# Moving the step projections of layer 0 from states 2 and 5 to states 5 and 8 of a pass, and the x and gate projections one place on

## The chip, the cores and the metric

The kernel runs on one core of a Trainium2 chip. The metric is the device time of one execution in microseconds, as the median of several runs. The engines are PE (TensorE, matmul), DVE (VectorE), ACT (ScalarE), POOL (GpSimd) and SP (SyncE, which here only issues DMAs). Each engine works through its own instruction list in the order written in the program, and waits on semaphores that other engines or DMAs raise.

## The reference, cut to what matters

The input is x of 8 images, 32 by 32 pixels, 192 channels. Two layers follow one another, each with a residual. The change touches layer 0 alone:

```
xz = groupnorm(x) @ W_in.T;  xc, z = split(xz)        # 384 channels each
xc = silu(depthwise_conv3x3(xc) + conv_b)
for each of 8 scan orders k (rows, columns, mirrored, reversed):
    x_dbl  = xs[k] @ x_proj_weight[k].T               # 12 step values, 16 B, 16 C per pixel
    delta  = softplus(dts @ dt_projs_weight[k].T + bias)   # 12 -> 384 channels
    h[t]   = exp(delta[t]*A) * h[t-1] + delta[t]*u[t]*B[t] # 16 states n, 1024 steps t
    y     += sum over n of h[t,n]*C[t,n]  + D*u
y = layernorm(y) * silu(z);  out = y @ W_out.T
```

The product dts @ dt_projs_weight is called step projection below, xs @ x_proj_weight the x projection, and the z half of the input projection the gate projection. Layer 1 is a scan of another form with four directions and isn't changed.

## The kernel before, in words

The images follow one another. Channels lie on the 128 partitions in J = 3 tiles, the 1024 pixels along the free axis, all in 32-bit floats. For layer 0 an image has 8 scans (i) of 3 tiles (j) of 16 states (n): 384 units, `UNITS`, numbered g. The 16 units of one (i, j) are a pass; an image has 24.

For each unit: SP fetches the row of B, broadcast to 128 partitions, into one of four buffers (`spread_row`, L312). POOL multiplies it with delta*u (`source`, L1043) into one of five buffers. ACT makes the decay exp(delta*A) in PSUM (`decay`, L825). DVE scans (`scan`, L1212). Then the state is multiplied by C: in 12 of 16 states by DVE (`weigh`, L1220), for which PE first spreads the row of C over the partitions in the two PSUM banks `WORK` (`spread_c`, L526); in states 2, 5, 8 and 11 (`by_pool`) by POOL (L1052), with a row of C that SP fetches. PE adds the product to the pass's sum by a matmul with the identity (`sum_states`, L556), and after a pass ACT copies the sum to y (`collect`, L831); at state 1 of the next pass PE reads y back into the sum (`begin_sums`, L544). In scan 0, DVE does that copy (L1225).

DVE's order is scan(g), then weigh(g-1) where that is DVE's. POOL's is source(g), then its weigh(g-3) where that is POOL's, and after source(6) of each pass `du` (L1033), two products that make delta*u of the next pass. POOL's source(g) waits for scan(g-5), whose buffer it takes, and for the row of B.

`WORK` is free in the four states whose C product is POOL's, since PE spreads no row for them. There PE does the projections, in pieces that `piece(g)` names. It is read by PE (`scans0` of the tensor block) at unit g, and by ACT at unit g+2, after decay(g+2), for the copy out of PSUM:

- ("dt", i, j): the step projection of the pass two on (`dt_proj`, L498; two matmuls of 12 rows and 512 columns, four in the trace), copied by `take_dt` (L802). Its softplus is at state 14.
- ("xd", i+1, q): a quarter of the next scan's x projection (`x_proj`), copied by `take_xd` (L777), after the fourth one `first_part`. The table `QUARTERS` has their places.
- ("rest", i+1, h): `remainders`, at states 8 and 11 of tile 2.
- ("z", j, h): the gate projection, in scan 7 alone. The table `GATES` has its places.

PE does a piece at unit g after it has waited for weigh(g-1), and before the sum of the state g-1 and the spread of g+1.

SP's list (`rows0`) goes by units too. At unit g it waits for source(g-4) to end and fetches B of g, and C of g if that is POOL's. At (0, 8) of scans 0 to 5, that is tile 0, state 8, after the rows of state 8, it waits for the step projection ("dt", i, 2) and then issues `load_wx(i + 2)`: two DMAs (L302, L303) which overwrite the weights that this projection was the last to read. At (2, 2) it stores the rows of the next scan's B and C to memory (`store_bc`).

Of the kernel before, what the change touches and what calls it, by code (L numbers as in the profile page):

```python
# [26 lines left out]
PASSES = K * J  # L27
# [25 lines left out]

QUARTERS = [(0, 5), (0, 8), (0, 11), (1, 2)]
GATES = {(0, 5): (0, 0), (0, 8): (0, 1), (0, 11): (1, 0), (1, 2): (1, 1), (1, 5): (2, 0), (1, 8): (2, 1)}


def last_xd(l, i):  # L60
# [4 lines left out]
def piece(g):  # L65

    if not 0 <= g < len(UNITS):
        return None
    i, j, n = UNITS[g]
    ahead = i * J + j + 2  # L70
    if n == (5 if j == 1 else 2) and ahead < PASSES:
        return "dt", ahead // J, ahead % J
    if i < K - 1 and (j, n) in QUARTERS:
        return "xd", i + 1, QUARTERS.index((j, n))
    if i < K - 1 and j == 2 and n in (8, 11):
        return "rest", i + 1, int(n == 11)
    if i == K - 1 and (j, n) in GATES:
        return "z", *GATES[j, n]
    return None
# [63 lines left out]
def program(nc, counts, images, x, out, w_in, conv_w, conv_b, w_x0, w_dt0, dt_b0, a_log0, d0,  # L143
# [3 lines left out]
    with ctx:  # L147
# [244 lines left out]
        def _(pe):  # L392
# [167 lines left out]
            def put_off(g):  # L560
                p = piece(g)
                return p is not None and p[0] == "rest"

            def scans0(b):
                for g in range(len(UNITS) + 1):
                    last = g - 1
                    if 0 <= last < len(UNITS) and not by_pool(*UNITS[last]):
                        pe.wait_ge(S["weigh"], at("weigh", UNITS[last], b))
                    p = piece(g)
                    if p:  # L570
                        if p[0] == "xd":
                            x_proj(b, p[1], p[2])
                        elif p[0] == "dt":
                            dt_proj(b, 0, p[1], p[2])
                        elif p[0] == "rest":
                            remainders(b, p[1], p[2])
                        else:
                            gate_projection(b, 0, p[1], p[2])
                    if g < len(UNITS) and not by_pool(*UNITS[g]):
                        spread_c(b, *UNITS[g])  # L580
                    if g >= SUM_LAG and by_pool(*UNITS[g - SUM_LAG]):
                        sum_states(b, g - SUM_LAG)

                    n = UNITS[g][2] if g < len(UNITS) else N
                    if n == 1:
                        begin_sums(b, last)
                    if n in (2, 3) or g >= 2 and put_off(g - 1):
                        sum_states(b, g - 2)
                    if 0 <= last and n not in (1, 2) and not put_off(g) and not by_pool(*UNITS[last]):
                        sum_states(b, last)  # L590
# [120 lines left out]
        def _(act):  # L711
# [121 lines left out]
            def scans0(b):  # L833
                for g in range(len(UNITS) + 2):
# [10 lines left out]
                    if g in (1, 2) and b > 0:  # L845
                        take_out1(b - 1, g - 1)
                    p = piece(g - 2)
                    if p and p[0] == "xd":
                        take_xd(b, 0, p[1], p[2])
# [627 lines left out]
```

## Time and profile before

| | us |
|---|---|
| median of 3 runs | 15642.82 |
| lowest and highest | 15638.57, 15650.55 |
| profiled execution: span from first to last instruction | 15638.3 |
| DVE busy | 14604.3 (93%) |
| POOL busy | 13820.4 (88%) |
| PE busy | 12948.2 (83%) |
| ACT busy | 8897.0 (57%) |
| DMA, share of 16 engines | 45.9% |
| mean granted TensorE clock | 0.946 |

The profile page gives no time for the profiled execution but its span; it lies within the three runs. Busy time is what an engine spends in instructions of its own. An image takes an eighth of the span; image 3 begins its layer 0 at 5912.1 and has 1222 us of it.

### The profile page before, as it was taken

Reading aid. Unit: us, or ns where it says so; the run is one execution under the profiler, and the core shown is the slowest. Engines: PE = TensorE matmul, PEld = TensorE weight load, DVE = VectorE, ACT = ScalarE, POOL = GpSimd, SP = SyncE. Lnnn points to the kernel's source line nnn. Section 1 sums busy time; section 2 is a strip of 40 time slices with the busy share of each in tenths; the row PEclk is TensorE's granted clock in tenths of the full one; section 3 lists DMA queues with packets and bytes.
Section 4 is the critical chain, followed back from the end, with each engine's and each line's share of the span. In section 5 each row is a group of like instructions: output and inputs, shape, how many; then the busy total and the mean of one; then the engine's idle time right before and its main releaser. Section 6 shows DMA issues by size and latency. Waiting matters only on the chain.

```text
span 15638.3 us, 128313 instructions
## 1 busy us (share of the span) xinstructions
PE 12948.2 (83%) x42560; PEld 7615.4 (49%) x42560; DVE 14604.3 (93%) x8593; ACT 8897.0 (57%) x8571; POOL 13820.4 (88%) x5892
## 2 busy tenths in 40 slices
PE   7887888878888788887888878888788887888878
PEld 4553355533555335553355533555335553355533
DVE  8998989989899899998999989999899998999988
ACT  4455745457454674556744567445674456744567
POOL 7997979979799798997989978899788997889978
PEclk8999999999999999999999999999999999999999
DMA  5662256622566225662256622566225662256622
GB/s 180 211 214 104 86 180 213 211 101 86 185 212 211 100 84 187 214 210 98 82 193 212 210 95 81 193 213 213 93 78 199 213 211 92 76 200 213 211 87 77
DMA packets 696921, 2473.06 MB, mean 158 GB/s; under 512 B 79292, under 2 KB 101064, under 8 KB 696264
## 3 DMA queue, kind: packets, MB, share of 16 engines
q1 hardware_dynamic: 696264, 2464.85, 45.9%
q8 instruction: 345, 5.65, 0.2%
q14 instruction: 312, 2.56, 0.1%
HBM read 2448.81 MB, written 15.73 MB: 158 GB/s over the span
## 4 chain that ended last, share of the span: by engine, by line
POOL 47%; issue 18%; DVE 13%; PE 11%; DMA 7%; ACT 3%; DVEq 0%; POOLq 0%; SPq 0%; ACTq 0%
POOL room L1043 24%; POOL room L1086 7%; DMA room<-bc_rows 7%; POOL room L1052 5%; POOL room L1078 4%; POOL room L1089 4%; DVE room L1279 4%; DVE room L1212 3%; PE bank L621 3%; POOL room L1033 3%; DVE room L1220 3%; PE bank L556 2%; PE bank L407 2%; DVE u L1169 1%; DVE room L1299 1%
## 5 line engine op out<-in xcount | busy, mean ns | idle before, releaser
L1043 POOL TENSOR_TENSOR room<-room 128x1024 f32<-128x1024 f32 x3072 | 7161.8, 2369 | 0.6
L1212 DVE TENSOR_TENSOR_SCAN room<-bank,room 128x1024 f32<-128x1024 f32 x3072 | 6936.5, 2278 | 75.7 <-POOL room L1043 71.7
L556 PE MATMUL bank<-room,identity 128*128 128x256 f32 x24576 | 5985.2, 389 | 188.5 <-DVE room L1220 188.5
L556 PEld LDWEIGHTS bank<-room,identity 128*128 128x128 f32 x24576 | 4758.9, 195 | 1333.5 <-DVE room L1220 269.6
L825 ACT ACTIVATE bank<-room,a 128x1024 f32<-128x1024 f32 x3072 | 3411.3, 1115 | 3273.9 <-DVE room L1212 3258.4
L621 PE MATMUL bank<-room,identity 128*128 128x512 f32 x6144 | 3011.5, 641 | 860.8 <-DVE room L1299 728.4
L1279 DVE TENSOR_TENSOR_SCAN room<-bank,room 128x1024 f32<-128x1024 f32 x1536 | 3431.5, 2274 | 54.1 <-POOL room L1086 33.6
L1220 DVE TENSOR_TENSOR room<-room,bank 128x1024 f32<-128x1024 f32 x2304 | 2764.1, 1200 | 387.3 <-PE bank L526 374.1
L621 PEld LDWEIGHTS bank<-room,identity 128*128 128x128 f32 x6144 | 1204.8, 204 | 2667.3 <-issue 1257.2
L1086 POOL TENSOR_TENSOR room<-room 128x1024 f32<-128x1024 f32 x768 | 2224.3, 2919 | 56.2 <-ACT room L908 26.7
L1052 POOL TENSOR_TENSOR room<-room 128x1024 f32<-128x1024 f32 x768 | 1817.1, 2366 | 344.1 <-DVE room L1212 343.0
L526 PE MATMUL bank<-parts,pick_row 96*128 96x512 bf16 x4608 | 1391.8, 383 | 806.7 <-DVE room L1220 702.4
L908 ACT ACTIVATE room<-room,a 128x1024 f32<-128x1024 f32 x1248 | 1365.9, 1138 | 4.5
L1089 POOL TENSOR_TENSOR room<-room 128x1024 f32<-128x1024 f32 x480 | 1160.5, 2428 | 0.0
L526 PEld LDWEIGHTS bank<-parts,pick_row 96*128 96x128 bf16 x4608 | 384.5, 99 | 1409.8 <-DVE room L1220 1079.0
L1033 POOL TENSOR_TENSOR room<-room,u 128x512 f32<-128x512 f32 x384 | 544.4, 1443 | 577.3 <-ACT room L808 577.3
L1078 POOL TENSOR_TENSOR room<-u,room 128x1024 f32<-128x1024 f32 x384 | 970.9, 2528 | 8.0 <-DMA room<-bc_rows 8.0
L600 PE MATMUL bank<-room,identity 128*128 128x512 f32 x1536 | 721.8, 592 | 0.0
L897 ACT ACTIVATE bank<-room,a 128x1024 f32<-128x1024 f32 x384 | 429.0, 1117 | 452.6 <-DVE room L1279 451.1
L498 PE MATMUL bank<-xdbl,wdt 12*128 12x512 f32 x864 | 488.1, 694 | 192.2 <-DVE room L1220 173.9
L1028 POOL TENSOR_TENSOR u<-room,u 128x1024 f32<-128x1024 f32 x24 | 56.6, 2356 | 651.3 <-ACT room L813 651.3
L918 ACT ACTIVATE bank<-room,a 128x1024 f32<-128x1024 f32 x288 | 320.6, 1113 | 383.6 <-DVE room L1279 383.6
(115 smaller groups left out, 8767.1 us busy)
## 6 DMA issues: line engine op xcount, KB each, us to landing
room<-bc_rows SPq DMA_DIRECT2D x4608, 512.0 KB, 4.4
wx<-in_w_x SPq DMA_DIRECT2D x65, 162.0 KB
bc_rows<-xdbl SPq DMA_DIRECT2D x72, 128.0 KB, 5.3
pictures<-in_x SPq DMA_DIRECT2D x8, 768.0 KB, 10.9
out_x<-pictures SPq DMA_DIRECT2D x8, 768.0 KB, 7.2
win<-in_w_in SPq DMA_DIRECT2D x16, 288.0 KB, 6.1
room<-in_w_in SPq DMA_DIRECT2D x16, 288.0 KB, 5.0
room<-in_w_out SPq DMA_DIRECT2D x16, 288.0 KB, 5.6
```

The lines of the kernel that those rows point to most:

```text
L526: ins = nc.tensor.matmul(bank[:, WORK[h], :], pick_row[:, N + n:N + n + 1].broadcast_to([XR, P]), parts[:, i % 2, halves(h)], start=True, ...
L556: ins = nc.tensor.matmul(dst[line][part], identity[:, :], src[line][part], start=(i == 0 and n == 0 and line == 0), stop=(n == N - 1 and l ...
L621: ins = nc.tensor.matmul(dst, identity[:, :], rhs, start=(q == 0), stop=(q == Q - 1))
L825: nc.scalar.activation(whole(DECAY0[g % 2]), delta0[:, j, :], ACT.Exp, scale=a0[:, col:col + 1]).then_inc(S["decay"], note("decay", (i, j, ...
L1043: nc.gpsimd.tensor_tensor(source0[:, g % SOURCES, :], du0[:, j, :], b_ring0[:, g % BROWS, :], ALU.mult).then_inc(S["source"], note("source ...
L1052: nc.gpsimd.tensor_tensor(state, state, c_ring0[:, c, :], ALU.mult).then_inc(S["weigh_pool"], note("weigh_pool", (i, j, n)))
L1078: nc.gpsimd.tensor_tensor(src, u[:, j, :], b_ring1[:, m % BROWS1, :], ALU.mult).then_inc(S["source1"], note("source1", (j, n)))
L1086: nc.gpsimd.tensor_tensor(state, state, src.rearrange("p (r c) -> p c r", r=SIDE), ALU.mult).then_inc(S["gated"], note("gated", (j, n, q)))
L1089: nc.gpsimd.tensor_tensor(state, state, src, ALU.mult).then_inc(S["gated"], note("gated", (j, n, q)))
L1212: nc.vector.tensor_tensor_scan(run(state0[:, g % STATES, :]), run(whole(DECAY0[g % 2])), run(source0[:, g % SOURCES, :]), 0.0, ALU.mult, A ...
L1220: nc.vector.tensor_tensor(state, state, whole(WORK[0]), ALU.mult).then_inc(S["weigh"], note("weigh", UNITS[g]))
L1279: nc.vector.tensor_tensor_scan(state, dec, state, 0.0, ALU.mult, ALU.add).then_inc(S["scan1"], note("scan1", (j, n, q)))
```

## The change

The step projections of tiles 0 and 2 go from state 2 to 5, that of tile 1 from 5 to 8. The quarters of the x projection and the six gate projections each go to the next place of the list. No computation is added or removed.

```diff
-QUARTERS = [(0, 5), (0, 8), (0, 11), (1, 2)]
-GATES = {(0, 5): (0, 0), (0, 8): (0, 1), (0, 11): (1, 0), (1, 2): (1, 1), (1, 5): (2, 0), (1, 8): (2, 1)}
+QUARTERS = [(0, 8), (0, 11), (1, 2), (1, 5)]
+GATES = {(0, 8): (0, 0), (0, 11): (0, 1), (1, 2): (1, 0), (1, 5): (1, 1), (1, 8): (2, 0), (1, 11): (2, 1)}
...
     ahead = i * J + j + 2
-    if n == (5 if j == 1 else 2) and ahead < PASSES:
+    if n == (8 if j == 1 else 5) and ahead < PASSES:
         return "dt", ahead // J, ahead % J
```

Places taken, by state, before and after:

| tile | before | after |
|---|---|---|
| 0 | 2 dt, 5 8 11 xd | 5 dt, 8 11 xd |
| 1 | 2 xd, 5 dt | 2 5 xd, 8 dt |
| 2 | 2 dt, 8 11 rest | 5 dt, 8 11 rest |

## Rows read from the trace of the kernel before

**Rows 1.** The page: busy engines, and one group of instructions with its idle time.

```profile
PE 12948.2 (83%) x42560; PEld 7615.4 (49%) x42560; DVE 14604.3 (93%) x8593; ACT 8897.0 (57%) x8571; POOL 13820.4 (88%) x5892
...
L1220 DVE TENSOR_TENSOR room<-room,bank 128x1024 f32<-128x1024 f32 x2304 | 2764.1, 1200 | 387.3 <-PE bank L526 374.1
```

**Rows 2.** Windows: stretch, its length, busy us of PE, PEld, DVE, ACT, POOL; clock; DMA.

```profile
6090.60:6839.10 748.50, 639.12 (x2580) 444.84 (x2580) 731.49 (x423) 373.57 (x380) 733.14 (x330) 0.98 0.62 212
...
6839.10:6989.30 150.20, 128.46 (x516) 89.46 (x516) 146.05 (x86) 77.11 (x79) 147.94 (x67) 0.98 0.61 211
...
8033.30:8788.10 754.80, 646.01 (x2580) 448.42 (x2580) 731.44 (x422) 373.44 (x380) 733.89 (x330) 0.97 0.61 210
...
6739.20:6787.90 48.70, 39.92 (x166) 28.24 (x166) 48.56 (x29) 24.72 (x25) 47.69 (x22) 1.00 0.61 211
```

**Rows 3.** Timeline of DVE, image 3, scan 5, tile 0: start, length, line, count.

```profile
6688.86 2.28 DVE L1212 TENSOR_TENSOR_SCAN room<-bank,room 128x1024 f32<-128x1024 f32 x1
...
6705.04 1.22 DVE L1220 TENSOR_TENSOR room<-room,bank 128x1024 f32<-128x1024 f32 x1 [1.78 <-PE bank L526]
...
6708.38 1.20 DVE L1220 TENSOR_TENSOR room<-room,bank 128x1024 f32<-128x1024 f32 x1
...
6735.91 2.28 DVE L1212 TENSOR_TENSOR_SCAN room<-bank,room 128x1024 f32<-128x1024 f32 x1
...
6739.22 2.28 DVE L1212 TENSOR_TENSOR_SCAN room<-bank,room 128x1024 f32<-128x1024 f32 x1
```

**Rows 4.** Timeline of POOL: the same pass, last row from scan 3.

```profile
6680.29 16.27 POOL L1043 TENSOR_TENSOR room<-room 128x1024 f32<-128x1024 f32 x7
6697.92 2.36 POOL L1052 TENSOR_TENSOR room<-room 128x1024 f32<-128x1024 f32 x1 [1.36 <-DVE room L1212]
...
6702.54 3.03 POOL L1033 TENSOR_TENSOR room<-room,u 128x512 f32<-128x512 f32 x2
...
6712.44 7.04 POOL L1043 TENSOR_TENSOR room<-room 128x1024 f32<-128x1024 f32 x3
...
6730.95 4.76 POOL L1043 TENSOR_TENSOR room<-room 128x1024 f32<-128x1024 f32 x2
...
6400.95 2.48 POOL L1033 TENSOR_TENSOR room<-room,u 128x512 f32<-128x512 f32 x2
```

**Rows 5.** Timelines of PE and SP, same pass, at state 2; then one window.

```profile
6698.99 1.97 PE L498 MATMUL bank<-xdbl,wdt 12*128 12x512 f32 x4 [0.59 <-DVE room L1220]
...
6700.99 0.33 SPq L302 DMA_DIRECT2D wx<-in_w_x  x1
...
6701.81 0.34 SPq L312 DMA_DIRECT2D room<-bc_rows  x1
...
6701.50:6704.50 3.00, 3.00 (x9) 2.25 (x8) 1.77 (x1) 2.65 (x3) 3.00 (x3) 0.55 0.73 145
```

**Rows 6.** State 5 of tile 1: timelines of DVE, PE (scan 5), then DVE elsewhere.

```profile
6756.85 1.20 DVE L1220 TENSOR_TENSOR room<-room,bank 128x1024 f32<-128x1024 f32 x1
...
6758.15 1.95 PE L498 MATMUL bank<-xdbl,wdt 12*128 12x512 f32 x4 [0.95 <-DVE room L1220]
...
318.57 1.22 DVE L1220 TENSOR_TENSOR room<-room,bank 128x1024 f32<-128x1024 f32 x1 [1.82 <-PE bank L526]
...
14251.38 1.22 DVE L1220 TENSOR_TENSOR room<-room,bank 128x1024 f32<-128x1024 f32 x1 [1.82 <-PE bank L526]
```

**Rows 7.** DMA view at the first row behind the weights: size, us to landing.

```profile
room<-bc_rows SPq DMA_DIRECT2D x1, 512.0 KB, 4.1
...
room<-bc_rows SPq DMA_DIRECT2D x1, 512.0 KB, 4.7
...
room<-bc_rows SPq DMA_DIRECT2D x1, 512.0 KB, 5.4
```

**Rows 8.** Timeline of DVE, image 3, scan 0, state 3 of tiles 1 and 2.

```profile
5998.55 1.22 DVE L1220 TENSOR_TENSOR room<-room,bank 128x1024 f32<-128x1024 f32 x1 [2.35 <-PE bank L526]
...
6055.61 1.22 DVE L1220 TENSOR_TENSOR room<-room,bank 128x1024 f32<-128x1024 f32 x1 [4.30 <-PE bank L526]
```

## The prediction

> **What bounds the kernel now.** I read the page first, then windows over whole scans, then the timelines of DVE, POOL, PE and SP side by side in one pass.
>
> The page shows DVE at 93% and POOL at 88% of the span, and one idle time of DVE that belongs to layer 0: 374.1 us in which the C product (L1220) waits for the spread row of C (L526) [rows 1]. The windows show how close the two engines are. Scan 6 of image 3 takes 150.20 us; DVE is busy for 146.05 of it and POOL for 147.94 [rows 2]. So layer 0 is bound by DVE plus 4.15 us of stalls for three passes, and POOL, which has only 2.26 us to spare, stands close behind. Whatever DVE gains beyond that, POOL takes back; and whatever delays POOL by more than its lead comes out at DVE.
>
> The timeline of one pass, scan 5, tile 0, shows the stall. The pass takes 6739.22 - 6688.86 = 50.36 us, with 1.78 in front of the product of state 3, so DVE's own pass is 48.58 [rows 3]. PE did the step projection from 6698.99 to 6700.96, and in the 3 us after 6701.50 its granted clock averaged 0.55, nearly all at the lower level, 1.2 GHz, after 0.59 us of idling and four matmuls of 12 rows [rows 5]. The sum of state 0 and the spread of state 3 come behind it on PE, at half speed. The pass with its step projection at state 5 took 48.70, with DVE busy 48.56: a stall of 0.14, its clock at 1.00 [rows 2]. So such a piece costs 0.14 at full clock and about 1.8 at half.
>
> POOL's own pass: source(15) of the pass before starts at 6680.29, so source(0) at 6682.60; source(15) starts at 6730.95, the next source(0) at 6733.26. Less 1.36 of waiting for scan(2), that is 49.3 us. `du` has 3.03 of it here and 2.48 in scans of rows and mirrored rows, where the pass is 48.8 [rows 4].
>
> **What the change removes.** The step projections at state 2 of tiles 0 and 2 go. In scans 3 to 6 nearly every one cost 1.78. With nothing at state 2, the spread of state 3 waits for the sum of state 0 alone, for which DVE leaves two scans' time: no stall. Tile 0 then goes to 48.6 for DVE before anything is added.
>
> **What it adds at states 5 and 8.** The same piece, of the same length, in front of the same sum and spread. The one before at state 5 of tile 1 is the nearest row: either 0.14, or 1.82 as in [rows 6]; of the 48 in scans 1 to 6 of eight images 15 had 1.82 (first and last shown). The bounds are none and all of them. I take 15 of 48, a share of 0.31, for every moved one, since it is the same place. DVE's passes:
> - tile 1: 48.58 + 0.14 = 48.7, below POOL's 48.8 or 49.3; or 48.58 + 1.82 = 50.4. Mean 0.69 x 48.8 + 0.31 x 50.4 = 49.3 in the first scans, and 49.6 with 49.3 for POOL in the later ones.
> - tile 2: scan 6 has 4.15 of stalls, of which 1.78 + 0.14 + 1.78 are step projections; 0.45 is left for the remainders. So 146.05 - 2 x 48.58 + 0.45 + 0.14 = 49.5, or 51.2; mean 50.0. Before it was 51.1 where halved.
>
> **What it adds on SP's queue.** This is the part that the diff doesn't show. At (0, 8) SP waits for the step projection of tile 2 before it issues the two weight loads, and all later rows of B and C queue behind that wait. Now PE ends it at 6700.96, SP issues the loads at 6700.99 and the row of state 9 at 6701.81 [rows 5], and source(9) starts at 6712.44 [rows 4]: hidden. Moved to state 5, the projection starts after weigh(4). Call the end of weigh(4) T. At state 5 of tile 1 the weigh ended at 6758.05 and the projection at 6760.10, so T + 2.05 [rows 6]. Then 0.03 to SP, 0.82 for two issues, and the landing of a row behind the weights: 4.7, the middle of the 55 rows of that kind, bounds 4.1 and 5.4 (shown are these three) [rows 7]. With 0.05 to wake, POOL can start source(9) at T + 7.65. Today it starts at 6712.44 - 6709.58 = T + 2.86 [rows 3, 4]; with T earlier by the 1.78 removed it would be about T + 4.6. So POOL loses 3 us here, more than its lead.
>
> From source(9) to source(15) are 18.51 us; scan(15) starts 2.41 later (2.36 for the source and 0.05), and the next scan(0) another 3.31 [rows 3, 4]. So the pass ends at T + 31.9, with T at 20.72 - 1.78 = 18.94 after scan(0): 50.8 us, where it now is 50.36 with a stall and 48.7 without. A halved clock at state 6 is hidden in it: scan(9) must wait to T + 10.1 anyway. The rows of states 10, 11 and 12 queue up too, but 213 GB/s at a share of 0.61 [rows 2] makes 1.5 us a row at full rate, faster than a source of 2.31.
>
> The Trainium skill ("DMA: Bandwidth & Descriptors", "Anatomy of one DMA") says that DMA engines don't wait on semaphores, the issuing sequencer does so before dispatch. The trace agrees: the row left SP only behind the loads.
>
> The same section puts a DMA at 2.0 us plus its bytes at 436 GB/s, fitted on the POOL-issued path; for 692 KB that is an estimate of 3.6 us rather than the 4.7 measured, and the sum below would be lower by 1.1 x 48 = 53 us, 15578. I go by the rows.
>
> **What else moves, at no cost.** The quarters of x at states 2 and 5 of tile 1: the pass that had a quarter at 2 and a step projection at 5 idled 0.14 in all, so a quarter costs nothing. ACT (57% busy) copies the step projection at state 7 or 10, before its softplus at 14, and no longer next to the copy of y at state 3. `store_bc` at (2, 2) waits for the last quarter, now at state 5 of tile 1, some 40 us ahead of use. If the ACT copy were late, it would show as a longer stall at the next product, at most one copy of 1.1 us.
>
> **The sum, for an image.** Scans 1 to 5 now: 748.50 in image 3 and 754.80 in image 4, mean 751.65 [rows 2]. After: scans 2 and 3, 50.8 + 49.3 + 50.0 = 150.1 each; scans 4 and 5, 50.8 + 49.6 + 50.0 = 150.4 each; scan 1 has DVE's last copy of y (731.49 - 5 x 146.05 = 1.2) more, 151.3. Together 752.3: +0.6. Scan 6 loads no weights: 49.6 + 49.6 + 50.0 = 149.2 for 150.2: -1.0. Scan 7, tile 0 alone: -0.8. Scan 0, tile 0: 31.9 from T for DVE's own 29.6, +2.3; tile 2: the stall of 4.30 [rows 8] goes, I put 0.3 in its place and 1.4 at state 5, where scan 0 halves more often, -2.6; tile 1 keeps its 2.35, for the quarter at state 2 stays. Sum 0.6 - 1.0 - 0.8 + 2.3 - 2.6 = -1.5, times 8 = -12 us. On the span of 15638.3 that is 15626; the median stands 4.5 above the span: 15631. The gain of about 3.4 us a scan from state 2 goes back to the new places of the stall and to SP's wait.
>
> **The rivals.**
> A. POOL's lead covers SP's wait, or the row comes much sooner. For: today's wait, equally long for the row, costs nothing. Against: T + 7.65 against T + 4.6. Then tile 0 would take 49.3 or 49.6 as tile 1 does: 1.5 less in scans 1 to 3, 1.2 in 4 and 5, 2.1 in 0; 9.0 an image, 72 us: 15559.
> B. The clock halves behind every moved projection, as it did in nearly all at state 2 of scans 3 to 6. Place: the products of state 9 in tile 1 and state 6 in tile 2. Price: tile 1 +1.1 or +0.8, tile 2 +1.1; in scans 1 to 5 4.8 + 5.7, in 6 and 7 3.5, so 14 an image, 112 us: 15743, slower. It decides from a share of about 0.57 on, where the time passes 15674. For: PE is emptier before state 5 than when a quarter stood at 2. Against: 33 of 48 at state 5.
> C. It halves behind none of them: tile 1 -0.5 or -0.3, tile 2 -0.5, in all 6.2 an image, 50 us: 15581.
> D. The row lands at 5.4: +0.7 x 48 = 34 us, 15665; at 4.1 29 us less.
>
> **How the numbers follow.** Forecast 0.47, A 0.12, B 0.18, C 0.18, D 0.05. What a measurement here can tell is 0.2%, 31 us. Faster (below 15612): A, C and 0.05 of the forecast's spread, 0.35. Slower (above 15674): B, 0.04 of the spread and most of D, 0.25. Same: 0.40. The forecast's own range, shares from 0.1 to 0.5 and landings of 4.4 to 5.0: 15595 to 15665. To leave out no more than 2 in 10 it goes down to 15562, just above A, and up to 15710, within B.
>
> **What would show it.** No stall in front of the product of state 3 in scans 2 to 6; stalls of 0.14 or 1.8 at state 6 of tile 2 and 9 of tile 1; in tile 0 of scans 0 to 5 POOL idle in front of source(9) until a row lands, 7.6 after weigh(4), and DVE then idle in front of scans 9 to 15 behind L1043, which it hardly is now. SP's weights 2.1 after weigh(4). Passes of 50.8, 49 and 50. It is wrong if POOL isn't idle there (A), or if PE's clock is low behind most of the moved pieces (B) or none (C).

## The result, and the profile after

The changed kernel is slower: 15706.36 us (median of 4 runs, 15697.92 to 15717.71) against 15645.6 for the kernel before (4 runs). The ratio is 1.0041, with a 95% interval of 1.0027 to 1.0054: 61 us lost where I forecast 12 gained. The time lies inside my range, but the likeliest case, no measurable change, did not happen. The profiled execution took 15714.33 us, 1.8 more than its span.

The page of the changed kernel, its span and four groups of instructions (busy us, mean ns, idle us and what ended most of it). The line of the engines and the one of L1220 answer to [rows 1]. Behind them stand three lines of the kernel before that [rows 1] doesn't show.

```profile
span 15712.5 us, 128298 instructions
...
PE 12977.8 (83%) x42560; PEld 7639.7 (49%) x42560; DVE 14626.1 (93%) x8593; ACT 8895.7 (57%) x8571; POOL 13818.4 (88%) x5892
...
L1043 POOL TENSOR_TENSOR room<-room 128x1024 f32<-128x1024 f32 x3072 | 7155.4, 2363 | 188.5 <-DMA room<-bc_rows 155.6
L1212 DVE TENSOR_TENSOR_SCAN room<-bank,room 128x1024 f32<-128x1024 f32 x3072 | 6940.8, 2277 | 138.1 <-POOL room L1043 72.8
...
L1220 DVE TENSOR_TENSOR room<-room,bank 128x1024 f32<-128x1024 f32 x2304 | 2759.0, 1197 | 379.9 <-PE bank L526 366.7
...
L1052 POOL TENSOR_TENSOR room<-room 128x1024 f32<-128x1024 f32 x768 | 1814.5, 2363 | 234.1 <-DVE room L1212 232.5
```
```profile
L1043 POOL TENSOR_TENSOR room<-room 128x1024 f32<-128x1024 f32 x3072 | 7161.8, 2369 | 0.6
L1212 DVE TENSOR_TENSOR_SCAN room<-bank,room 128x1024 f32<-128x1024 f32 x3072 | 6936.5, 2278 | 75.7 <-POOL room L1043 71.7
...
L1052 POOL TENSOR_TENSOR room<-room 128x1024 f32<-128x1024 f32 x768 | 1817.1, 2366 | 344.1 <-DVE room L1212 343.0
```

Two things are seen at once. POOL's sources, which had waited 0.6 us in all, now wait 188.5, and 155.6 of it is put down to a row that a DMA brings. POOL gets 110 of this back at its own C products (L1052), where it now waits 234.1 in place of 344.1: a part of the new wait only takes the place of an old one. At DVE the idle time before the scans (L1212) grew from 75.7 to 138.1. POOL is named for only 72.8 of it, for 71.7 before; of the added 62 us 40.1 stand as "issue" and 18.9 behind ACT's decay (L825), below as waits with us in total, times and longest. The 1.05 in front of scan(9) in the timeline further down is such an "issue": source(9) had ended just before, so the name is a weak guide there.

```profile
DVE room L1212 <- issue: 40.1, 70, 2.1
DVE room L1212 <- ACT bank L825: 18.9, 54, 1.0
```

And the wait of DVE for the spread row, 374.1 us before, is 366.7: the stall that the change was to shorten is still there, only in other places. Nearly the same amount of it, plus a new wait, is most of the result.

Windows of the changed kernel: scans 1 to 5 and scan 6 of image 3, scans 1 to 5 of image 4. They answer to [rows 2].

```profile
6102.60:6867.10 764.50, 650.80 (x2580) 451.30 (x2580) 733.41 (x423) 373.12 (x380) 735.83 (x331) 0.97 0.60 209
6867.10:7017.30 150.20, 128.52 (x516) 89.29 (x516) 146.03 (x86) 77.10 (x79) 147.57 (x67) 0.98 0.60 210
8061.90:8827.30 765.40, 651.03 (x2580) 451.23 (x2580) 733.86 (x423) 373.35 (x380) 736.42 (x332) 0.97 0.60 209
```

Scans 1 to 5 take 765 where they took 748.5 and 754.8, and where I forecast 752.3; in the mean of the eight images it is 761.1 for 751.3. Scan 6, which loads no weights, takes 150.20 as before in image 3; in the mean of the eight images it went from 149.85 to 150.95, where I had forecast 149.2. POOL and DVE are busy for about as long as before (DVE 733.41 us for 731.49 in image 3); nearly all of the loss is idle time.

The timelines of POOL, SP, PE and DVE in scan 3, tile 0 of image 3, around the rows of state 9. They answer to [rows 3 to 5].

```profile
6423.90 4.66 POOL L1043 TENSOR_TENSOR room<-room 128x1024 f32<-128x1024 f32 x2
6428.52 2.36 POOL L1052 TENSOR_TENSOR room<-room 128x1024 f32<-128x1024 f32 x1
6434.26 6.99 POOL L1043 TENSOR_TENSOR room<-room 128x1024 f32<-128x1024 f32 x3 [3.38 <-DMA room<-bc_rows]
```
```profile
6428.68 0.33 SPq L302 DMA_DIRECT2D wx<-in_w_x  x1
6429.05 0.40 SPq L303 DMA_DIRECT2D wdt<-in_w_dt  x1
6429.50 2.81 SPq L312 DMA_DIRECT2D room<-bc_rows  x5
```
```profile
6426.70 1.95 PE L498 MATMUL bank<-xdbl,wdt 12*128 12x512 f32 x4 [0.95 <-DVE room L1220]
```
```profile
6407.77 2.28 DVE L1212 TENSOR_TENSOR_SCAN room<-bank,room 128x1024 f32<-128x1024 f32 x1
...
6425.40 1.19 DVE L1220 TENSOR_TENSOR room<-room,bank 128x1024 f32<-128x1024 f32 x1
...
6436.70 4.61 DVE L1212 TENSOR_TENSOR_SCAN room<-bank,room 128x1024 f32<-128x1024 f32 x2 [1.05 <-issue]
...
6458.55 2.28 DVE L1212 TENSOR_TENSOR_SCAN room<-bank,room 128x1024 f32<-128x1024 f32 x1
```

weigh(4) ends at 6426.59, the step projection at 6428.65, SP issues the weights at 6428.68 and then five rows without a pause, the backlog of states 9 to 12. source(9) starts at 6434.26, 7.67 after weigh(4) (forecast 7.65), after 3.38 of idling, and scan(9) at 6436.70, after 1.05. The pass ends at 6458.55. It began at 6407.77, so it took 50.8 us, the forecast to a tenth.

### The profile page after: what moved, and what is told of

Its sections match the earlier page's. It is cut to its first block, busy times and chain, and to the rows that moved or that the text cites. A ratio compares the mean times of both kernels' runs of the same rounds, so it can differ in the third digit from the quotient of the medians.

```text
span 15712.5 us, 128298 instructions
## 1 busy us (share of the span) xinstructions
PE 12977.8 (83%) x42560; PEld 7639.7 (49%) x42560; DVE 14626.1 (93%) x8593; ACT 8895.7 (57%) x8571; POOL 13818.4 (88%) x5892
## 4 chain that ended last, share of the span: by engine, by line
POOL 46%; issue 17%; DVE 12%; PE 12%; DMA 9%; ACT 3%; SPq 0%; DVEq 0%; POOLq 0%; ACTq 0%
POOL room L1043 24%; DMA room<-bc_rows 9%; POOL room L1086 7%; POOL room L1052 4%; POOL room L1078 4%; POOL room L1089 4%; DVE room L1279 3%; PE bank L621 3%; DVE room L1212 2%; POOL room L1033 2%; DVE room L1220 2%; PE bank L556 2%; PE bank L407 2%; DVE u L1169 1%; PE bank L498 1%
## 5 line engine op out<-in xcount | busy, mean ns | idle before, releaser
L1043 POOL TENSOR_TENSOR room<-room 128x1024 f32<-128x1024 f32 x3072 | 7155.4, 2363 | 188.5 <-DMA room<-bc_rows 155.6
L1212 DVE TENSOR_TENSOR_SCAN room<-bank,room 128x1024 f32<-128x1024 f32 x3072 | 6940.8, 2277 | 138.1 <-POOL room L1043 72.8
L825 ACT ACTIVATE bank<-room,a 128x1024 f32<-128x1024 f32 x3072 | 3411.3, 1115 | 3373.3 <-DVE room L1212 3364.0
L1220 DVE TENSOR_TENSOR room<-room,bank 128x1024 f32<-128x1024 f32 x2304 | 2759.0, 1197 | 379.9 <-PE bank L526 366.7
L1052 POOL TENSOR_TENSOR room<-room 128x1024 f32<-128x1024 f32 x768 | 1814.5, 2363 | 234.1 <-DVE room L1212 232.5
## 6 DMA issues: line engine op xcount, KB each, us to landing
out_x<-pictures SPq DMA_DIRECT2D x8, 768.0 KB, 10.8
```

What stands on the lines that cost most here:

```text
L825: nc.scalar.activation(whole(DECAY0[g % 2]), delta0[:, j, :], ACT.Exp, scale=a0[:, col:col + 1]).then_inc(S["decay"], note("decay", (i, j, ...
L1043: nc.gpsimd.tensor_tensor(source0[:, g % SOURCES, :], du0[:, j, :], b_ring0[:, g % BROWS, :], ALU.mult).then_inc(S["source"], note("source ...
L1052: nc.gpsimd.tensor_tensor(state, state, c_ring0[:, c, :], ALU.mult).then_inc(S["weigh_pool"], note("weigh_pool", (i, j, n)))
L1212: nc.vector.tensor_tensor_scan(run(state0[:, g % STATES, :]), run(whole(DECAY0[g % 2])), run(source0[:, g % SOURCES, :]), 0.0, ALU.mult, A ...
L1220: nc.vector.tensor_tensor(state, state, whole(WORK[0]), ALU.mult).then_inc(S["weigh"], note("weigh", UNITS[g]))
```

## The experiments

One measure is used throughout. A stall in front of the product that follows a step projection is called long over 1 us; with 12 rows nearly all of the others are 0.13 or 0.14. I counted long ones in scans 1 to 6 of eight images, 48 for each tile, and their sum with the short ones. "before" and "changed" are the two kernels of the case. Each count comes from the one profiled execution of its kernel. e1 to e4, e5 to e8 and e9 have each their own runs of the kernel before, so ratios are compared.

| kernel | us | ratio to before (95%) | long, tiles 0, 1, 2 | of 144 | stall, us an image |
|---|---|---|---|---|---|
| before | medians 15642 to 15650 | 1 | 43, 15, 30 | 88 | 20.7 |
| changed | 15706.36 | 1.0041 (1.0027 to 1.0054) | 26, 33, 34 | 93 | 23.4 |
| e1 changed, loads late | 15648.11 | 0.9999 (0.999 to 1.0008) | 32, 8, 48 | 88 | 21.9 |
| e2 before, loads late | 15647.68 | 1.0002 (0.9993 to 1.0011) | 44, 16, 33 | 93 | 22.3 |
| e3 before, long wait of SP | 15725.55 | 1.0047 (1.0035 to 1.006) | 36, 28, 26 | 90 | 20.3 |
| e4 changed, 108 rows | 15541.01 | 0.9933 (0.992 to 0.9945) | 0, 0, 0 | 0 | 0 |
| e5 before, 108 rows | 15434.96 | 0.9866 (0.9853 to 0.988) | 0, 0, 0 | 0 | 0 |
| e6 changed, 108 rows, loads late | 15420.24 | 0.9858 (0.9844 to 0.9871) | 0, 0, 0 | 0 | 0 |
| e7 before, tile 2 at state 5 | 15569.41 | 0.9953 (0.994 to 0.9965) | 27, 19, 29 | 75 | 17.0 |
| e8 e1, tile 2 back at state 2 | 15565.8 | 0.9951 (0.9938 to 0.9965) | 13, 13, 7 | 33 | 9.0 |
| e9 e1, pause of 0.27 us | 15629.63 | 0.9988 (0.9979 to 0.9997) | 29, 18, 41 | 88 | 23.5 |
| e9 e1, pause of 0.49 us | 15658.87 | 1.0008 (0.9999 to 1.0016) | 39, 33, 29 | 101 | 25.9 |
| e9 e1, pause of 0.91 us | 15673.78 | 1.0017 (1.0008 to 1.0026) | 43, 23, 11 | 77 | 19.7 |

In the profiles with 108 rows DVE has no idle time at all at these places in scans 1 to 6.

**SP's wait: e1, e2 and e3.** e1 and e2 move the wait and the two loads behind the rows of state 12, e1 in the changed kernel, e2 in the kernel before:

```diff
-                    if (j, n) == (0, 8) and i + 2 < K:
+                    if (j, n) == (0, 12) and i + 2 < K:
                         sp.wait_ge(S["mm"], at("mm", ("dt", 0, i, J - 1), b))
                         load_wx(i + 2)
```

> The changed kernel, with SP's wait for the step projection and the two weight loads moved from behind the rows of state 8 to behind those of state 12. My theory: of the 61 us that the change lost, SP's wait is a part of its own, since it starves POOL before source(9) in scans 0 to 5 (3.9 us idle on average, 1.2 us a scan of it reaching DVE in tile 0 of scans 1 to 5). Without it tile 0 goes from 51.0 to about 49.6, some 9 us an image: 72 us faster than the changed kernel, about 15635, the time of the kernel before. POOL has no idle time before source(9), and the shares of long stalls behind the step projections stay above half. Rival: SP's wait is covered and the longer stalls on PE explain all; then the time stays within 20 us of 15706.

> The kernel before, with the same move of wait and loads to behind state 12. In it the row of state 9 lands well before use, so by both theories nothing changes: within 15 us of the kernel before. If it gets faster by 30 us or more, SP's wait had a cost in the kernel before too, and the comparison of e1 has to be corrected by it.

e3 does the opposite in the kernel before: nothing of PE's work moves, and SP waits at the old place for something that ends later.

```diff
-                        sp.wait_ge(S["mm"], at("mm", ("dt", 0, i, J - 1), b))
+                        sp.wait_ge(S["mm"], at("mm", ("xd", 0, i + 1, 0), b))
```

> The kernel before, with every piece in its old place, but at tile 0, state 8, SP waits for the x projection's quarter at state 5 in place of the step projection at state 2. That ends about 1.1 us after weigh(4), so source(9) can start about 6.6 us after it where it now starts 2.9 after it. My theory: POOL idles 3 us or more there, the pass goes from 50.4 to about 51.3, so 40 to 60 us slower, about 15695, with no piece of PE's work moved. Rival, the wait is covered by POOL's lead: within 15 us of before.

e1 came back to the time of the kernel before (0.9999), e2 did not differ from it (1.0002), and e3 was slower by 0.47%, more than the 40 to 60 us expected. What POOL waited for, in the changed kernel, then in e3 (us in total, times, longest); e1 has no line for L1043:

```profile
POOL room L1043 <- DMA room<-bc_rows: 155.6, 41, 8.8
```
```profile
POOL room L1043 <- DMA room<-bc_rows: 186.3, 43, 6.2
```

So SP's wait by itself is enough for a loss of this size. Taking it out of the changed kernel gives back 58 us of 61 by the medians, and putting one into the kernel before costs 0.47% with every piece in its place. Neither is quite a clean measure, since the long stalls change too (93 to 88, and 88 to 90); e4 against e6, below, has none of them. This also means that moving the projections, without the queue, gained nothing: e1 is no faster than the kernel before. That is the second question.

**The rows of the matmul: e4, e5 and e6.** The step projection's matmuls contract 12 rows. These kernels contract 108: the whole of `xdbl`, against weights whose first 96 rows are zero, set once at the start. Columns and instructions are the same.

```diff
-                w = wdt[XR:XR + R, i % 2, :] if l == 0 else wdt1[XR:XR + R, :]
+                lo = 0 if l == 0 else XR
+                w = wdt[:, i % 2, :] if l == 0 else wdt1[XR:XR + R, :]
...
-   w[:, j * P:(j + 1) * P], xdbl[XR:XR + R, halves(h)],
+   w[:, j * P:(j + 1) * P], xdbl[lo:XR + R, halves(h)],
...
+            nc.vector.memset(wdt[0:XR, :, :], 0.0).then_inc(setup, 1)
...
```

> The changed kernel, with the step projection of layer 0 done over 108 rows in place of 12: the 96 rows more of the weights are zero, so the result is the same, and the number of columns and instructions too. My theory: PE's clock falls behind the step projection because its matmuls have 12 rows. Then stalls of about 1.8 us and more behind it (26 of 48 in tile 0, 33 in tile 1, 34 in tile 2 of scans 1 to 6) go down to 0.14, some 17 us an image: about 135 us faster than the changed kernel, 15570; SP's wait stays. Rival: the clock falls because PE idles before the piece, or by when it comes; then the shares stay and the time is within 20 us of 15706.

> The kernel before, all pieces in their old places, with the step projection of layer 0 over 108 rows, 96 of them zero weights. My theory: the long stalls behind it are the low clock's, 88 of 144 projections of scans 1 to 6 in the kernel before; at 0.14 each DVE needs 48.7, 48.7 and 49.5 for the three passes and POOL's own 48.8 or 49.3 sets the pace. Scans 1 to 5 go from 751 to about 740, the others lose 8 together: 19 us an image, 150 us faster than before, about 15490. Rival: state 2 is a bad place in itself (the copy of y on ACT, begin_sums on PE), so that stalls stay there with a full clock; then it is no faster than the changed kernel with 108 rows (15541).

> The changed kernel with both: 108 rows, and SP's wait and weight loads behind the rows of state 12. My theory: what is left of the change is only the place, and it is worth nothing once the clock stays up and the queue is free, since POOL sets the pace: tile 0 goes from 50.9 to 49.3, 10 us an image, 75 us faster than with 108 rows alone, about 15465 to 15490, and within 25 us of the kernel before with 108 rows. Rival: the new places are better in themselves, then it is 40 us or more faster than that kernel.

PE's timeline at state 5 of tile 2 (the piece, the sum behind it, the spread), and a window over the 3 us behind the piece, whose last three numbers are granted clock, DMA share and GB/s. First e1, with 12 rows, then e4, with 108.

```profile
6797.01 2.08 PE L498 MATMUL bank<-xdbl,wdt 12*128 12x512 f32 x4 [0.95 <-DVE room L1220]
6799.02 3.51 PE L556 MATMUL bank<-room,identity 128*128 128x256 f32 x8
6802.37 0.60 PE L526 MATMUL bank<-parts,pick_row 96*128 96x512 bf16 x2
```
```profile
6799.00:6802.00 3.00, 3.00 (x8) 2.44 (x8) 2.29 (x2) 2.71 (x3) 3.00 (x2) 0.50 0.98 340
```
```profile
6812.27 1.96 PE L499 MATMUL bank<-xdbl,wdt 108*128 108x512 f32 x4 [0.95 <-DVE room L1221]
6814.06 1.89 PE L557 MATMUL bank<-room,identity 128*128 128x256 f32 x8
6815.79 0.60 PE L527 MATMUL bank<-parts,pick_row 96*128 96x512 bf16 x2
```
```profile
6814.00:6817.00 3.00, 3.00 (x15) 2.40 (x14) 3.00 (x3) 2.44 (x3) 3.00 (x2) 1.00 0.72 269
```

PE idles 0.95 us before either piece, and the piece takes nearly as long (2.08 and 1.96). Behind 12 rows the clock is at 0.50, 1.2 GHz, and eight sums take 3.51 us; behind 108 it stays at 1.00 and they take 1.89. No long stall is left in scans 1 to 6 of any of the three kernels. So in these scans it takes the 12 rows to bring the clock down: the 0.59 or 0.95 us of idling before the piece isn't enough without them. Whether 12 rows would do it without the idling, no run shows. Nor does state 2 have a fault of its own in these scans: e5, with everything at the old places, is the faster of e4 and e5.

Scan 0 is different. There PE idles about 4 us before the piece at state 2 of tile 2, and with 108 rows too the clock is low during the piece, which takes 3.29 us for 1.96, and DVE still stalls for 1.79 us, as image 3 of e5 shows:

```profile
5964.42 3.29 PE L499 MATMUL bank<-xdbl,wdt 108*128 108x512 f32 x4 [4.02 <-DVE room L1221]
```
```profile
5970.34 1.22 DVE L1221 TENSOR_TENSOR room<-room,bank 128x1024 f32<-128x1024 f32 x1 [1.79 <-PE bank L527]
```

All eight images have such a stall of 1.79 us or more; before they had 3.6 to 4.3. In e4 and e6, with the piece at state 5, PE has idled about 0.8 us before it and there is no stall. So longer idling is followed by the low clock without the 12 rows, and here the new place is the better one.

With the clock out of the way the queue is seen alone. e4 against e5 is the whole change at full clock: 106 us slower. e6 against e4 is SP's wait: 121 us. e6 against e5 is the places alone: 15 us faster. The intervals overlap, but the four runs of each do not (15418 to 15425 and 15432 to 15437), and scan 0 has the gain: there tile 2 takes 50.5 us for 52.4. Windows over scans 1 to 5 of image 3, e4 then e6; in the second POOL is busy nearly throughout:

```profile
6046.40:6793.30 746.90, 624.74 (x2580) 438.75 (x2580) 734.31 (x422) 374.12 (x380) 733.20 (x330) 1.00 0.61 213
```
```profile
5995.70:6730.80 735.10, 623.34 (x2580) 437.65 (x2580) 731.68 (x422) 373.56 (x380) 733.60 (x330) 1.00 0.62 216
```

My expectations for e4 and e5 were too cautious by 29 and 55 us: for e5 I had put scans 1 to 5 at 740 and they took 735, and I had left scan 0 its old stalls. e6 came out 45 us below the lower end of what I wrote: I had priced SP's wait at 75 us there, and it was 121.

**Place or timing: e7, e8 and e9.** With 12 rows, what decides how often the clock falls? e7 moves only tile 2's projection, in the kernel before; e8 takes only tile 2's move back, in e1.

```diff
-    if n == (5 if j == 1 else 2) and ahead < PASSES:
+    if n == (5 if j >= 1 else 2) and ahead < PASSES:      # e7
...
-    if n == (8 if j == 1 else 5) and ahead < PASSES:
+    if n == (5, 8, 2)[j] and ahead < PASSES:              # e8
```

> The kernel before with tile 2's step projection alone at state 5; 12 rows, SP's wait as before. Theory 1: how often the clock falls is not a property of the place; in four kernels with different places 88, 88, 93 and 90 of the 144 projections of scans 1 to 6 had a long stall, though the share of a single tile went from 8 to 48 of 48. Then again 75 to 100 of 144 are long, at whichever tile, and the time is within 20 us of before. Theory 2, that of my prediction: state 5 has the share of 15 of 48 that tile 1 had there; then tile 2's falls from 30 to about 15, tile 1's stays, and it is about 25 us faster. Theory 3: state 5 after an empty state 2 has a share of 0.7; then about 20 us slower, with 34 in tile 2 and 15 in tile 1.

> The changed kernel with the weight loads behind state 12, and tile 2's step projection back at state 2; tiles 0 and 1 as changed. In e1 tile 2 had a long stall in 48 of 48, tile 0 in 32 and tile 1 in 8. Theory 1: the total stays between 75 and 100 of 144 and the time within 20 us of e1 (15648), while the shares of tiles 0 and 1, which aren't touched, change. Theory of places: tiles 0 and 1 keep 32 and 8, tile 2 goes back to about 30 as in the kernel before; then 18 fewer, about 30 us faster than e1.

Both were about 80 us faster than their base, and no theory had the time of either right; theory 1 had the total of e7, at its lowest. The total is not constant: 75 in e7, 33 in e8. But the shares are no property of the place either. In e8 tiles 0 and 1 were not touched and went from 32 and 8 to 13 and 13, and tile 2, back at the place where it had 30 in the kernel before, has 7. In e3, where no piece had moved, tile 1 went from 15 to 28. An empty state 2 doesn't decide it either: tile 2 at state 5 had 48 in e1 and 29 in e7. And within one execution the same piece falls both ways: in scan 2, tile 0 of the kernel before, four images have a long stall and four have none. What is left is when the piece comes. That is what e9 tries: e1 with one DVE instruction that nobody reads, once a scan, some 29 us ahead of tile 2's piece.

```diff
                         scan(b, g)
                         i, j, n = UNITS[g]
+                        if i > 0 and (j, n) == (1, 12):
+                            nc.vector.memset(room[:, 7, 0:256], 0.0)     # 512, 1024
```

> The changed kernel with the loads behind state 12 (e1), plus one DVE memset of 256 columns that nothing reads, at state 12 of tile 1 of scans 1 to 7: a pause of some tenths of a us, 56 times, and no piece of PE's work moved. e1 had long stalls in 32, 8 and 48 of 48 in tiles 0, 1 and 2. Theory of timing: whether the clock falls behind a step projection depends on when it comes, so the pause changes the counts, at tile 2 above all, and the time need not grow; by the spread of the kernels so far (33 to 93 of 144) it may lie anywhere from 15560 to 15720. Theory of places (an emptier state 2 makes state 5 worse): 32, 8 and 48 stay, and the time is that of e1 plus 56 pauses, 15655 to 15680.

> As the one with 256 columns, with 512: twice the pause. Theory of timing: other counts again, in no order with the length of the pause. Theory of places: the counts of e1, and 10 to 30 us above the one with 256 columns.

> As the one with 256 columns, with 1024: four times the pause, at most 1.2 us, 67 us in all. Theory of timing: other counts again; below e1 plus 67 us where they are lower. Theory of places: the counts of e1, and about 15690 to 15715.

The pauses took 0.27, 0.49 and 0.91 us, 56 times each (15.2, 27.2 and 51.1 us in all). Tile 2's long stalls went from 48 to 41, 29 and 11, tile 1's from 8 to 18, 33 and 23. No projection had moved. With the shortest pause the kernel was not slower than e1 (0.9988, interval 0.9979 to 0.9997, against 0.999 to 1.0008), with the longest it lost 26 us of the 51 that were put in. The middle one came out 29 us above the shortest, as the theory of places had it, but with other counts. That bears out timing and speaks against places. What in the timing decides, I can't say from these runs, and I could not have predicted any of the counts; tile 2's fell in order with the pause, which I had not expected.

The counts are not the same in every execution either. The runs of a kernel with 12 rows spread over 21 to 40 us, those of one with 108 rows over 4 to 11 us, and the execution counted for the pause of 0.49 us took 24 us more than the median of its kernel. So 41 for 48 alone would prove little. 11 for 48 is far more than the kernel before and e2 differ by, in which no piece moved (43, 15, 30 and 44, 16, 33).

e7's 77 us are not explained by the counts alone: 3.7 us an image less stall in scans 1 to 6 is 30 us. Scan 0, whose pieces see a low clock more often, took 170.1 us in the mean where it took 174.1, another 32. The same holds for the shortest pause: it has no fewer long stalls than e1, and its scans 1 to 5 are longer, but scan 0 took 171.9 us for 174.9.

## Why the prediction was wrong, step by step

**Both engines nearly bind: right.** Once the stalls were gone (e6), scans 1 to 5 took 735.10 with DVE busy 731.68 and POOL 733.60.

**The stall at state 3 goes: right.** None is left in tiles 0 and 2 of scans 1 to 6; in scan 0, tile 2 has 0.43 for the 4.30 of [rows 8].

**SP's wait: right, with place and size.** 7.67 for 7.65, 50.8 for 50.8 in the pass shown, and 51.0 in the mean of scans 2 to 5 of all images. The row of state 9 landed 3.9 to 5.7 us after its issue in 48 cases, median 4.8, for the 4.7 that I took. I priced the wait at 72 us in rival A; e1 gives 58 with a low clock, e4 and e6 121 at full clock, when no stall covers any of it. POOL's lead doesn't cover it, so rival A is out. The estimate of 3.6 us by the Trainium skill ("DMA: Bandwidth & Descriptors", "Anatomy of one DMA") stays below every one of these landings; the rows were the better guide, and its sentence that the issuing sequencer does the waiting is what this trace shows once more: five rows left SP in 2.81 us, behind a wait that concerned none of them.

**The stalls at the new places: wrong, and this is the step that failed.** "I take 15 of 48, a share of 0.31, for every moved one, since it is the same place." It came out as 93 of 144, a share of 0.65, and 67 of 96 in the two tiles where SP's wait doesn't hide it. I also held the size at 1.82; in tiles 1 and 2 the long ones were 2.0 us in the mean, up to 2.99. In those two tiles the term was 0.66 us a projection (0.69 x 0.14 + 0.31 x 1.82), 12 projections an image in scans 1 to 6: 7.9 us. It measured 17.4. The difference, 9.4 us an image, is 75 us, and my forecast was 75 too low. The passes say nearly the same: tiles 1 and 2 of scans 1 to 6 took 605.5 us an image where I forecast 596.7, which is 71 us in eight images. That is rival B: I had said that it decides from a share of 0.57 on, with 112 us for a share of 1. At 0.70 that line gives 15631 + 112 x 0.39 / 0.69 = 15694; 15706 was measured. e1 shows this step without SP's wait: rival A put such a kernel at 15559 with the share of 0.31, and it took 15648, with 88 of 144.

That 15706 still lies inside the range is no merit of the mechanism: the upper end was put at 15710 to leave out no more than 2 in 10, and so reaches into rival B. The forecast's own range, with shares of 0.1 to 0.5, ended at 15665.

The mistake was to read a share as belonging to a place. The kernel before had 88 of 144 over its three places, 0.61, and with the same matmuls in the same number there was no row that promised fewer. Taking that share for all three would have given 15631 + 112 x 0.30 / 0.69 = 15680, slower. e3, e8 and e9 show why the 15 of 48 meant nothing: the same place had 28 in e3, and tile 2 had 48, 41, 29 and 11 in e1 and the three kernels of e9, with the piece unmoved. What would have let me forecast the share of 0.65, or any other, stays open.

**Rival C**, no halving at the new places, would have needed what e4 to e6 made.

**Quarters, ACT, `store_bc` at no cost: right as far as seen.** At state 6 of tile 1, now behind a quarter, no stall is listed, and e6 has no new wait of POOL or DVE.

## What to carry to other kernels

Before a producer is moved, list every queue that waits for its result, and what is queued behind that wait: here two small loads held back five rows of another consumer, and moving the wait four states down in the list undid all of the loss. A stall that comes and goes at one place in the program need not be a property of that place, and here it was none; take its share over all places with the same instruction, and look for what in the instruction causes it. Here that was a matmul of 12 rows, and filling it up with zero rows, at no cost in instructions, was worth more (1.34% in the kernel before) than any order of the pieces tried here; with the late loads it gave the fastest version, e6, 1.42% below the kernel before.

## What the runs showed of the hardware

- Behind four matmul instructions of 12 rows by 512 columns, 1.95 us in all after 0.59 or 0.95 us of idling, the granted clock fell from 1.00 to 0.50 in 88 of 144 cases of the kernel before; behind the same four with 108 rows it never did so in scans 1 to 6 of three kernels. After 4.02 us of idling it was low with 108 rows too (scan 0 of e5). The number of rows doesn't change their duration (1.95 and 1.96 us).
- Whether it falls behind a given 12-row piece can be shifted by less than 1 us of unrelated work on another engine, 29 us earlier: 48 of 48 became 41, 29 and 11 with 0.27, 0.49 and 0.91 us. Against e1 the total moved by -0.11, +0.09 and +0.18%, where the pauses themselves add up to 0.10, 0.17 and 0.33%. An experiment on it that changes anything else at the same time says little unless the stalls are counted.
- Five broadcast rows of 512 KB issued back to back landed one after another, the first 3.9 to 5.7 us after its issue and the fifth 8.1 to 10.8; in the pass shown POOL waited only for the first.
